# A graph network stack on one core: three-plane table blocks for the second spline layer, and the third layer's table built in the stage that finds the targets

## The chip, the cores and the metric

The kernel runs on one core of one Trainium2 chip. The metric is the device time in microseconds of one execution; lower is better.

## The reference

Four graph layers follow each other on 6250 nodes (32 features) and 100000 edges, each added to its input and layer-normed. The change touches only the first, a spline convolution with a small network that shifts the edge coordinates:

```python
def spline_basis(pseudo):               # [E, 3] in [0, 1], 5 knots a dimension
    pos = pseudo * (KS - 1)
    i0 = jnp.clip(jnp.floor(pos), 0, KS - 2)
    frac = pos - i0
    ...                                 # 8 corner weights and 8 indices into 125 knots
def spline_conv(x, row, col, basis, idx, W, b):
    z = jnp.einsum('ni,kio->nko', x, W).reshape(N * K, Fout)
    gathered = z[col[:, None] * K + idx]
    msg = jnp.einsum('es,eso->eo', basis, gathered)
    out = jax.ops.segment_sum(msg, row, num_segments=N)
    return out / jnp.maximum(deg, 1.0)[:, None] + b
h = elu(spline_conv(ones, row, col, basis, idx, stn1_w, stn1_b))   # 1 -> 64
h = elu(spline_conv(h, row, col, basis, idx, stn2_w, stn2_b))      # 64 -> 64
h = elu(h @ stn3_w + stn3_b)
t = h @ stn4_w + stn4_b
new_pseudo = clip(pseudo + t[col] - t[row], 0.0, 1.0)
basis2, idx2 = spline_basis(new_pseudo)
return spline_conv(x, row, col, basis2, idx2, conv_w, conv_b)      # 32 -> 32
```

## The kernel before

Nodes are padded to 6272 (49 tiles of 128, in 7 batches of 7), edges to 100352 (784 columns of 128, one edge a partition and column). The stages run one after the other; each is a block in which every engine has its own program, and semaphores order them. For the spline layer they are, in order of time:

- **Basis sweep.** The first 392 of 784 pair scatters run on GpSimd beside it. A pair scatter is an indirect DMA that writes 128 two-byte counts into a matrix in DRAM; later layers use it.
- **Table stage** (`stage_z` with `SplineTable`). For each node tile and each of the 5 planes of 25 knots, TensorE makes four pieces of a 128x1600 product in one of two four-bank PSUM buffers; VectorE copies pieces 0 and 2 to SBUF and ScalarE pieces 1 and 3; ScalarE then issues the store of that plane's block (800 KB, 6400 bytes a partition). Five blocks a tile, 245 stores, go to `z_stn2` (125 knots of 64 floats a node).
- **stn2 sweep** (`stage_spline_sweep` with chunks of 7 columns, in `summed_sweep`). GpSimd issues two indirect gathers a column, each of 7 consecutive knots (1792 bytes) an edge, from plane n and plane n+1. Two ring buffers alternate. VectorE weighs the 8 corners (`produce`), gives the ring back, and makes the segmented sums; ScalarE stages the gather indices when a ring comes free, spreads the decay and turns the sums for the store. Beside it the `PairTable` of the third layer is built: 56 tiles of 112 nodes, 5 planes each, two product pieces a plane on TensorE, two or four copies on ScalarE, and 224 stores of 700 KB that ScalarE issues into `z_conv`, where each row holds a knot and its neighbour in the next plane. In a sweep step of two chunks ScalarE does planes 0 to 2 after the first chunk and planes 3 and 4 after the second (`pairs.scalar`).
- **Target stage** (`stage_targets`). GpSimd issues the other 392 pair scatters. For each unit of 4 columns (7 a chunk of 28, 196 in all) TensorE counts and turns a one-hot matrix (`turn`, 8 matmuls), ScalarE copies the turned rows to SBUF as bf16 (`lo_rows`, L1834), TensorE looks the target values up (`look`, 12 matmuls), and VectorE picks them (L1795). `turned` and `found` have two PSUM buffers each, and `turn` of unit u is issued ahead of `look` of unit u-1.
- **conv sweep.** The same sweep with chunks of 28 columns and one gather of 1792 bytes an edge from `z_conv`.

The semaphores that matter below: `lo_rows_ready` (ScalarE to TensorE), `turned_ready` (back), `found_ready` and `found_free` (with VectorE), `pair_plane` and `pair_free` (TensorE and ScalarE around a plane of the pair table), `indices_staged` (ScalarE to GpSimd), `ring_free` (VectorE to ScalarE).

Of the kernel before, what the change touches and what calls it, by code (L numbers as in the profile page):

```python
# [5 lines left out]
I32 = mybir.dt.int32  # L6
BF16 = mybir.dt.bfloat16
F16 = mybir.dt.float16
ALU = mybir.AluOpType
# [5 lines left out]
P = 128  # L15


def gnn_stack_kernel(nc, t, out, stop=None):

    N, FX = t["x"].shape  # L20
# [13 lines left out]
    K3P = (KD - 1) * KD * KD  # L34
    H1 = t["L0_gnn_stn1_w"].shape[2]
# [58 lines left out]
    with ctx:  # L94
# [9 lines left out]
        z_stn2 = dram("z_stn2", [NP * K3, H1])  # L104
# [595 lines left out]
        def summed_sweep(gathers, ch, width, produce, dest, keep, tail, decay_in_psum=False, pool=None, pairs=None):  # L700

            steps = J // ch // 2
            with ExitStack() as st, nc.Block() as block:
# [27 lines left out]
                @block.tensor  # L731
                def _(pe):
                    if pairs:
                        pairs.tensor(pe)

                @block.sync
                def _(sp):
                    if pairs:
                        pairs.sync(sp)
# [15 lines left out]
                def _(a):  # L755
# [37 lines left out]
                    if pairs:  # L793
                        pairs.scalar_begin(a)
                    with a.Fori(0, steps - 1) as it:
                        for b in range(2):
                            chunk(b, it * (2 * ch) + (2 + b) * ch, it * (2 * ch) + (1 + b) * ch)
                            if pairs:
                                pairs.scalar(a, it, 3 * b, 3 + 2 * b, True)
                    chunk(0, None, J - ch)  # L800
                    if pairs:
                        pairs.scalar(a, steps - 1, 0, KD, False)
                    chunk(1, None, None)
                    if pairs:
                        pairs.scalar_end(a)
# [606 lines left out]
        def spline_setup(pseudo, w8, units, starts, dst_f):  # L1412


            with ExitStack() as st:
# [5 lines left out]
                def f(v):  # L1421
# [35 lines left out]
                    for d, s in enumerate((KD * KD, KD, 1)):  # L1457
# [3 lines left out]
                    v.tensor_copy(starts[0][:, :], ix[:, :]).then_inc(dve_step, 1)  # L1461
                    v.wait_ge(dve_step, 1)
                    v.sem_inc(dve_step, -1)
                    if len(starts) == 2:
                        v.tensor_scalar(starts[1][:, :], ix[:, :], float(KD * KD), None, ALU.add).then_inc(dve_step, 1)
                        v.wait_ge(dve_step, 1)
                        v.sem_inc(dve_step, -1)
                vector_stage(f)

        class PairTable:  # L1470

            def __init__(self, st, arr, kin, w_dram, fo, z):
                self.arr, self.kin, self.fo, self.w_dram = arr, kin, fo, w_dram
                self.nodes = NP // (J // SEVEN // 2)
                self.n_blocks = KD - 1
                self.zv = z.rearrange("(t p u) o -> p t u o", p=self.nodes, u=self.n_blocks * KD * KD)
                self.wsb = sb(st, "pair_w", [kin, K3, fo])
                self.flat = sb(st, "pair_x", [kin, NP])
                self.cell = sb(st, "pair_cell", [kin, self.nodes])
                self.blocks = [sb(st, f"pair_block{a}", [self.nodes, KD * KD, 2, fo]) for a in range(self.n_blocks)]  # L1480
                self.acc = [ps(st, f"pair_acc{n}", [P, 2, 512]) for n in range(2)]
                cuts = [0, KD * KD // 2, KD * KD]
                self.pieces = list(zip(cuts[:-1], cuts[1:]))
                self.stored = [counted(f"z_stored{a}") for a in range(self.n_blocks)]
                self.base = [k.base for k in self.stored]
                self.tiles = NP // self.nodes
                for k in self.stored:
                    k.base += 16 * (self.tiles + 1)
                self.turns = [(n, min(n + 8, NT)) for n in range(0, NT, 8)]

            def sync(self, sp):
                cut = [K3 * n // self.n_blocks for n in range(self.n_blocks + 1)]
                for a in range(self.n_blocks):
                    sp.dma_start(self.wsb[:, cut[a]:cut[a + 1], :],
                                 self.w_dram.rearrange("k i o -> i k o")[:, cut[a]:cut[a + 1], :]).then_inc(self.stored[a].sem, 16)

            def tensor(self, pe):
                for n, (lo, hi) in enumerate(self.turns):
                    if n >= 2:
                        pe.wait_ge(sem(f"pair_free{n % 2}"), 1)  # L1500
                        pe.sem_inc(sem(f"pair_free{n % 2}"), -1)
                    for k in range(lo, hi):
                        last = pe.transpose(self.acc[n % 2][0:self.kin, (k - lo) // 4, (k - lo) % 4 * P:((k - lo) % 4 + 1) * P],
                                            self.arr[:, k, :], ident[:, :])
                    last.then_inc(sem("pair_turned"), 1)
                for a in range(self.n_blocks):
                    pe.wait_ge(self.stored[a].sem, self.base[a] + 16)
                with pe.Fori(0, self.tiles):
                    pe.wait_ge(sem("pair_cell_ready"), 1)
                    pe.sem_inc(sem("pair_cell_ready"), -1)  # L1510
                    for plane in range(KD):
                        g = plane % 2
                        pe.wait_ge(sem(f"pair_free{g}"), 1)
                        pe.sem_inc(sem(f"pair_free{g}"), -1)
                        for n, (lo, hi) in enumerate(self.pieces):
                            cols = self.wsb[:, plane * KD * KD + lo:plane * KD * KD + hi, :].rearrange("i k o -> i (k o)")
                            last = pe.matmul(self.acc[g][0:self.nodes, n, 0:(hi - lo) * self.fo], self.cell[:, :], cols, start=True, stop=True)  # L1517
                        last.then_inc(sem("pair_plane"), 1)
                for g in range(2):
                    pe.wait_ge(sem(f"pair_free{g}"), 1)  # L1520
                    pe.sem_inc(sem(f"pair_free{g}"), -1)

            def next_cell(self, a, tile):
                a.copy(self.cell[:, :], self.flat[:, bass.ds(tile * self.nodes, self.nodes)]).then_inc(act_step, 1)
                a.wait_ge(act_step, 1)
                a.sem_inc(act_step, -1)
                a.sem_inc(sem("pair_cell_ready"), 1)

            def scalar_begin(self, a):
                for n, (lo, hi) in enumerate(self.turns):  # L1530
                    a.wait_ge(sem("pair_turned"), 1)
                    a.sem_inc(sem("pair_turned"), -1)
                    for k in range(lo, hi, 4):
                        w = min(4, hi - k) * P
                        last = a.copy(self.flat[:, k * P:k * P + w], self.acc[n % 2][0:self.kin, (k - lo) // 4, 0:w])
                    last.then_inc(act_step, 1)
                    a.wait_ge(act_step, 1)
                    a.sem_inc(act_step, -1)
                    a.sem_inc(sem(f"pair_free{n % 2}"), 1)
                self.next_cell(a, 0)  # L1540

            def scalar(self, a, tile, first, end, more):
                for plane in range(first, end):
                    if plane < self.n_blocks:
                        a.wait_ge(self.stored[plane].sem, tile * 16 + (16 + self.base[plane]))
                        a.sem_inc(act_step, 1)
                        a.wait_ge(act_step, 1)
                        a.sem_inc(act_step, -1)
                    a.wait_ge(sem("pair_plane"), 1)
                    a.sem_inc(sem("pair_plane"), -1)  # L1550
                    for slot in range(2):
                        if 0 <= plane - slot < self.n_blocks:
                            for n, (lo, hi) in enumerate(self.pieces):
                                last = a.copy(self.blocks[plane - slot][:, lo:hi, slot, :],  # L1554
                                              self.acc[plane % 2][0:self.nodes, n, 0:(hi - lo) * self.fo].rearrange("p (u o) -> p u o", o=self.fo))
                    last.then_inc(act_step, 1)
                    a.wait_ge(act_step, 1)
                    a.sem_inc(act_step, -1)
                    a.sem_inc(sem(f"pair_free{plane % 2}"), 1)
                    if plane > 0:  # L1560
                        lo = (plane - 1) * KD * KD
                        a.dma_start(self.zv[:, bass.ds(tile, 1), lo:lo + KD * KD, :],
# [1624 lines left out]
```

## Time and profile before

| what | us |
| --- | --- |
| median of 2 runs | 11371.64 (11367.02 to 11376.25) |
| profiled execution, span from first to last instruction | 12824.6 |
| no other time of the profiled execution is recorded | |

Stages in the profiled execution: rank (sort) 340 to 1500, basis sweep 1577 to 2100, table 2238 to 2830, stn2 sweep 2871 to 5200, target stage 5384 to 6445, conv sweep 6500 to 7560. The rest is the attention layers and the matrix layers. Times in rows are microseconds unless marked ns. DMA is the mean busy share of the 16 DMA engines; PEclk is the granted clock of TensorE as a share of full speed, 0.50 being 1.2 GHz and 1.00 being 2.4 GHz. A row of windows has the stretch, its length, busy time (and count) of PE, PEld, DVE, ACT and POOL, then PEclk, DMA share and GB/s. In a row of groups the first number pair is busy us and mean ns, then the idle time before them with what ended it. A timeline row has start, duration, engine, line.

### The profile page before, as it was taken

How to read it: one execution, taken by the hardware profiler on the slowest of the kernel's cores; microseconds unless marked ns; L12 is line 12 of the kernel's file. 1: busy time of each engine (PE TensorE's matmuls, PEld its weight loads, DVE VectorE, ACT ScalarE, POOL GpSimd, SP SyncE). 2: the span in 40 equal slices, each digit the busy share in tenths (PEclk: the TensorE clock that was granted, in tenths of full speed). 3: DMA queues.
4: the chain of work that ended last, by engine and by line, in shares of the span. 5: the costliest groups of instructions: out<-in, count | busy, mean ns of one | idle time of the engine just before them, and what ended most of it. 6: DMA issues, size and time to landing. Idle time of an engine off the chain costs nothing. (4 is left out here: it accounts for less than half of the span.)

```text
span 12824.6 us, 84874 instructions
## 1 busy us (share of the span) xinstructions
PE 3493.7 (27%) x19713; PEld 2186.6 (17%) x19713; DVE 5436.1 (42%) x7001; ACT 2482.3 (19%) x3625; POOL 6756.2 (53%) x6784
## 2 busy tenths in 40 slices
PE   4344201763333333303500010001000100005877
PEld 3222101331111111302500000001000100004544
DVE  5333485444454444303754442222222377773111
ACT  0222152432222222101200001111111134430000
POOL 2666475006666666573057767776777566661000
PEclk8555555985555555556755555555555555557899
DMA  6000021877777777200046641111111123335799
GB/s 272 2 3 3 12 106 63 345 295 230 240 238 231 238 233 233 64 0 0 0 134 188 176 108 36 34 33 27 36 33 33 26 73 93 95 98 186 320 386 360
DMA packets 587391, 1693.59 MB, mean 132 GB/s; under 512 B 268075, under 2 KB 322770, under 8 KB 569201
## 3 DMA queue, kind: packets, MB, share of 16 engines
q0 software_dynamic: 292720, 608.23, 18.6%
q1 hardware_dynamic: 230560, 722.30, 14.5%
q10 hardware_dynamic: 63952, 361.30, 7.6%
q8 instruction: 56, 0.92, 0.0%
q14 instruction: 103, 0.84, 0.0%
HBM read 1016.07 MB, written 675.24 MB: 132 GB/s over the span
## 5 line engine op out<-in xcount | busy, mean ns | idle before, releaser
L1997 POOL DMA_INDIRECT ring<-tab_gat,at x2352 | 2347.4, 998 | 928.3 <-issue 835.5
L724 POOL DMA_INDIRECT ring<-z_stn,at x1568 | 1514.8, 966 | 1506.8 <-POOLq L721 991.1
L724 POOL DMA_INDIRECT ring<-z_conv,at x784 | 794.3, 1013 | 853.9 <-POOLq L721 592.9
L1517 PE MATMUL pair_acc<-pair_w,pair_cell 32*112 32x384 f32 (+1 forms) x1120 | 806.0, 887 | 1499.7 <-issue 468.9
L578 POOL DMA_INDIRECT sorted<-rows,at x784 | 800.8, 1021 | 710.6 <-POOLq L576 477.3
L1100 POOL DMA_INDIRECT adj<-val_a,at_a x784 | 785.5, 1002 | 335.0 <-issue 255.7
L2576 PE MATMUL acc<-spot,ones 128*128 128x128 f32 x6 | 2.3, 487 | 3444.1 <-PEq L1965 2243.5
L1267 PE MATMUL acc<-tile,parts 128*96 128x448 f16 (+1 forms) x3430 | 728.5, 361 | 254.4 <-DVE parts L1191 139.2
L1916 DVE COPY corner_banks<-w 128x56 f32 (+1 forms) x140 | 35.7, 255 | 1549.5 <-issue 389.7
L2108 DVE COPY peak<-peak 128x6 f32<-128x6 f32 x112 | 21.4, 191 | 1567.3 <-DMA ring<-tab_gat,at 1521.1
L1517 PEld LDWEIGHTS pair_acc<-pair_w,pair_cell 32*112 32x112 f32 x1120 | 307.8, 295 | 1996.9 <-issue 1996.9
L2576 PEld LDWEIGHTS acc<-spot,ones 128*128 128x128 f32 x6 | 1.5, 311 | 3444.8 <-issue 3444.8
L1554 ACT COPY pair_block<-pair_acc 112x384 f32<-112x384 f32 (+1 forms) x896 | 380.8, 502 | 896.9 <-issue 438.7
L2144 DVE TENSOR_TENSOR_SCAN sums<-decay,sums 128x1176 f32<-128x1176 f32 (+1 forms) x112 | 517.3, 4619 | 29.0 <-issue 11.4
L1267 PEld LDWEIGHTS acc<-tile,parts 128*96 128x96 bf16 (+1 forms) x3430 | 403.1, 125 | 573.7 <-DMA tile<-adj 239.2
L2032 ACT ACTIVATE weights_bank<-arg 128x168 f32<-128x168 f32 (+1 forms) x112 | 31.3, 279 | 2414.3 <-issue 1966.3
L2131 DVE TENSOR_TENSOR sums<-ring,weights_bank 128x1008 f32<-128x1008 f32 (+1 forms) x112 | 430.1, 3841 | 143.5 <-issue 108.4
L1173 POOL DMA_INDIRECT own<-tab_gcn,ex_src x5 | 5.0, 991 | 907.8 <-DMA tab_gcn<-hop 601.9
L2047 ACT COPY out_rows<-sums 128x1176 f32<-128x1176 f32 (+1 forms) x112 | 443.0, 3956 | 48.9 <-ACTq L2046 16.6
L1637 PE MATMUL planes<-wsb,turned 64*128 64x384 f32 (+1 forms) x1960 | 421.5, 537 | 72.8 <-PEq L1633 72.8
L1795 DVE TENSOR_TENSOR prod<-found,hot_hi 128x588 f32<-128x588 f32 x196 | 151.1, 771 | 644.2 <-remote 306.9
L836 DVE TENSOR_TENSOR_SCAN sums<-decay,sums 128x448 f32<-128x448 f32 (+2 forms) x168 | 387.9, 2309 | 43.2 <-issue 27.3
(510 smaller groups left out, 9794.9 us busy)
## 6 DMA issues: line engine op xcount, KB each, us to landing
tile<-adj SPq DMA_DIRECT2D x490, 784.0 KB, 21.4
z_stn<-block ACTq DMA_DIRECT2D x245, 800.0 KB, 4.9
z_conv<-pair_block ACTq DMA_DIRECT2D x224, 700.0 KB
run_gat<-out_rows SPq DMA_DIRECT2D x56, 1596.0 KB
adj<-zero SPq DMA_DIRECT2D x49, 1568.0 KB
run_basis<-out_rows SPq DMA_DIRECT2D x28, 1750.0 KB
ring<-tab_gat,at POOLq DMA_INDIRECT x2352
run_gat<-out_rows SPq DMA_DIRECT2D x56, 672.0 KB
```

What stands on the lines that cost most here:

```text
L578: g.indirect_dma_start(out=dest, out_offset=bass.IndirectOffsetOnAxis(ap=at[b][:, k:k + 1], axis=0), in_=rows[b][:, k, :], in_offset=None) ...
L724: g.indirect_dma_start(out=view(bufs[b], k), out_offset=None, in_=table, in_offset=bass.IndirectOffsetOnAxis(ap=at[n][b][:, k:k + 1], axis ...
L836: v.tensor_tensor_scan(flat, decay[:, :, :].rearrange("p f j -> p (f j)"), flat, 0.0, ALU.mult, ALU.add).then_inc(dve_step, 1)
L1100: g.indirect_dma_start(out=adj, out_offset=bass.IndirectOffsetOnAxis(ap=at_a[:, k:k + 1], axis=0), in_=val_a[:, k:k + 1], in_offset=None). ...
L1267: ins = pe.matmul(acc[0:3 * w, b, 0:HW_B], parts[:, t_, :, :].rearrange("p k f -> p (k f)"), self.ring[n % RING][:, b * HW_B:(b + 1) * HW_ ...
L1517: last = pe.matmul(self.acc[g][0:self.nodes, n, 0:(hi - lo) * self.fo], self.cell[:, :], cols, start=True, stop=True)
L1554: last = a.copy(self.blocks[plane - slot][:, lo:hi, slot, :], self.acc[plane % 2][0:self.nodes, n, 0:(hi - lo) * self.fo].rearrange("p (u ...
L1637: ins = pe.matmul(self.acc[g][:, n, 0:(hi - lo) * self.fo], self.turned[rows, k, :], cols, start=True, stop=True)
L1997: g.indirect_dma_start(out=ring[b][:, k, :], out_offset=None, in_=tab_gat, in_offset=bass.IndirectOffsetOnAxis(ap=at[b][:, k:k + 1], axis= ...
L2047: a.copy(out_rows[b][:, :, 0:n_sums], sums[b][:, :, :, :].rearrange("p h f j -> p j (h f)"))
L2131: v.tensor_tensor(sums[b][:, :, 1:per_head, :], val_of(ring[b]), ex.unsqueeze(2).to_broadcast([P, NH, width, ch]), ALU.mult)
L2144: v.tensor_tensor_scan(flat, decay[:, :, :, :].rearrange("p h f j -> p (h f j)"), flat, 0.0, ALU.mult, ALU.add).then_inc(dve_step, 1)
```

## The change

Two things change.

`z_stn2` is laid out in two blocks of three planes a node (planes 0, 1, 2 and planes 2, 3, 4), each knot's three planes side by side: 150 rows of 64 floats a node instead of 125. One gather of 20 consecutive rows (5120 bytes) holds all 8 corners of an edge, so there is one gather a column, 784 instead of 1568. The table stage drains plane 2 twice, into both blocks, and stores two blocks a tile of 2400 KB each (19200 bytes a partition) from two sets of SBUF blocks. `spline_setup` gets two more small VectorE instructions for the start rows.

The pair table leaves the sweep and is built in the target stage, with 49 tiles of 128 nodes. Its two product pieces use different 32-row groups of TensorE. It has one PSUM buffer of two banks, and `turned` and `keys` give up one bank each for it. SyncE issues its stores. ScalarE and TensorE take 35 planes an iteration of 28 units, in the written-out order below.

```diff
-        def summed_sweep(gathers, ch, width, produce, dest, keep, tail, decay_in_psum=False, pool=None, pairs=None):
+        def summed_sweep(gathers, ch, width, produce, dest, keep, tail, decay_in_psum=False, pool=None):
...
                     with a.Fori(0, steps - 1) as it:
                         for b in range(2):
                             chunk(b, it * (2 * ch) + (2 + b) * ch, it * (2 * ch) + (1 + b) * ch)
-                            if pairs:
-                                pairs.scalar(a, it, 3 * b, 3 + 2 * b, True)
...
 class PairTable
+            def tensor_plane(self, pe, n):
+                k, plane = divmod(n, KD)
+                pe.wait_ge(sem("planes_free0"), 1)
+                pe.sem_inc(sem("planes_free0"), -1)
+                for m, (lo, hi) in enumerate(self.pieces):
+                    rows = slice(m * self.kin, (m + 1) * self.kin)
+                    cols = self.wsb[rows, plane, 0:hi - lo, :].rearrange("i k o -> i (k o)")
+                    pe.matmul(self.acc[:, m, 0:(hi - lo) * self.fo], self.turned[rows, k, :], cols,
+                              start=True, stop=True).then_inc(sem("plane_for_act"), 1)
...
+            def scalar_plane(self, a, it, n):
+                k, plane = divmod(n, KD)
+                if plane < self.n_blocks:
+                    a.wait_ge(self.stored[plane].sem, it * (16 * TB) + (16 * k + self.start[plane]))
...
+                a.wait_ge(sem("plane_for_act"), 2)
+                a.sem_inc(sem("plane_for_act"), -2)
+                for slot in range(2):
+                    if 0 <= plane - slot < self.n_blocks:
+                        for m, (lo, hi) in enumerate(self.pieces):
+                            last = a.copy(self.blocks[plane - slot][:, lo:hi, slot, :],
+                                          self.acc[:, m, 0:(hi - lo) * self.fo].rearrange("p (u o) -> p u o", o=self.fo))
+                last.then_inc(act_step, 1)
+                a.wait_ge(act_step, 1)
+                a.sem_inc(act_step, -1)
+                a.sem_inc(sem("planes_free0"), 1)
+                if plane > 0:
+                    a.sem_inc(sem("pair_block_full"), 1)
...
 class SplineTable
-                self.blocks = [sb(st, f"block{a}", [P, KD * KD, self.slots, fo]) for a in range(self.n_blocks)]
+                self.blocks = [[sb(st, f"block{a}{e}", [P, KD * KD, SLOTS, fo]) for e in range(2)] for a in range(2)]
...
+            def places(self, plane):
+                return [(a, plane - 2 * a) for a in range(2) if 0 <= plane - 2 * a < SLOTS]
+            def drain(self, put, k, plane, first):
+                for a, slot in self.places(plane):
+                    for n, (lo, hi) in list(enumerate(self.pieces))[first::2]:
+                        last = put(self.blocks[a][k % 2][:, lo:hi, slot, :],
+                                   self.acc[(k * KD + plane) % 2][:, n, 0:(hi - lo) * self.fo].rearrange("p (u o) -> p u o", o=self.fo))
...
 stage_targets
-                turned = [ps(st, f"turned{b}", [P, UN, P]) for b in range(2)]
+                turned = ps(st, "turned", [P, UN, P])
...
+                def planes_after(n):
+                    return range(planes * n // (4 * units), planes * (n + 1) // (4 * units))
...
                 @block.scalar
+                    with a.Fori(0, steps // 2) as it:
+                        pairs.scalar_tiles(a, it)
+                        for n in range(4 * units):
+                            b, u = n // units % 2, n % units
+                            a.wait_ge(sem("turned_ready"), 1)
+                            a.sem_inc(sem("turned_ready"), -1)
+                            a.copy(lo_rows[b][:, u * UN:(u + 1) * UN, :], turned[:, :, :]).then_inc(act_step, 1)
+                            a.wait_ge(act_step, 1)
+                            a.sem_inc(act_step, -1)
+                            a.sem_inc(sem("lo_rows_ready"), 1)
+                            if n == 0:
+                                pairs.scalar_turned(a)
+                                a.sem_inc(sem("z_tiles_ready"), 1)
+                            for m in planes_after(n):
+                                pairs.scalar_plane(a, it, m)
...
                 @block.tensor
+                            for u in range(1, units + 1):
+                                rows_taken()
+                                if u < units:
+                                    turn(b, u)
+                                look(b, u - 1)
+                                if half == 0 and u == 1:
+                                    pe.wait_ge(sem("z_tiles_ready"), 1)
+                                    pe.sem_inc(sem("z_tiles_ready"), -1)
+                                for m in planes_after(half * units + u - 1):
+                                    pairs.tensor_plane(pe, m)
```

`rows_taken` is the wait for `lo_rows_ready` that stood at the head of `look` before.

## Rows read from the trace of the kernel before

**Rows 1.** The page: span, busy time of each engine.
```profile
span 12824.6 us, 84874 instructions
...
PE 3493.7 (27%) x19713; PEld 2186.6 (17%) x19713; DVE 5436.1 (42%) x7001; ACT 2482.3 (19%) x3625; POOL 6756.2 (53%) x6784
```

**Rows 2.** Windows: stages or their steady parts; columns as told above.
```profile
2238.00:2830.00 592.00, 433.56 (x2009) 218.07 (x2009) 253.70 (x493) 237.05 (x511) 0.00 (x0) 0.90 0.85 343
2300.00:2400.00 100.00, 78.61 (x367) 39.17 (x367) 45.69 (x90) 42.67 (x93) 0.00 (x0) 0.93 0.90 365
...
3000.00:5000.00 2000.00, 696.40 (x968) 266.08 (x968) 984.55 (x1262) 517.27 (x1208) 1313.45 (x1358) 0.50 0.76 236
5384.00:5910.00 526.00, 39.20 (x297) 31.38 (x297) 30.58 (x35) 8.20 (x14) 397.58 (x392) 0.51 0.02 0
5910.00:6445.00 535.00, 293.82 (x3625) 283.96 (x3625) 357.37 (x289) 106.71 (x182) 0.45 (x1) 0.77 0.00 0
...
6600.00:7500.00 900.00, 0.00 (x0) 0.00 (x0) 441.99 (x309) 67.57 (x69) 673.61 (x666) 0.50 0.65 182
```

**Rows 3.** Groups of instructions in the stn2 sweep, 2871 to 5200.
```profile
L724 POOL DMA_INDIRECT ring<-z_stn,at x1568 | 1514.8, 966 | 1506.8 <-POOLq L721 991.1 <-issue 509.0 <-remote 6.6
L1517 PE MATMUL pair_acc<-pair_w,pair_cell 32*112 32x384 f32 (+1 forms) x1120 | 806.0, 887 | 1499.7 <-issue 468.9 <-PEq L1514 392.1 <-remote 390.1
```

**Rows 4.** Waits in that stretch, us in total, times, longest.
```profile
POOL ring L724 <- POOLq L721: 991.1, 43, 710.4
```

**Rows 5.** One source line (ScalarE's `chunk_done` increment), both sweeps; ns min/median/max.
```profile
L785 ACTq EVENT_SEMAPHORE  x112: 4/17/1380, 2908.9 to 5197.7; - x112
```

**Rows 6.** The same line, conv sweep.
```profile
L785 ACTq EVENT_SEMAPHORE  x27: 17/17/17, 6563.0 to 7545.5; - x27
```

**Rows 7.** Timeline of ScalarE, target stage, while the scatters run: start, duration.
```profile
5399.38 0.59 ACT L1834 CAST lo_rows<-turned 128x512 bf16<-128x512 f32 x1 [1.91 <-issue]
...
5655.78 0.59 ACT L1834 CAST lo_rows<-turned 128x512 bf16<-128x512 f32 x1 [55.41 <-issue]
5711.78 0.59 ACT L1834 CAST lo_rows<-turned 128x512 bf16<-128x512 f32 x1 [55.41 <-ACTq L1833]
```

**Rows 8.** Line L1834 after the scatters, 5910 to 6445.
```profile
L1834 ACT CAST lo_rows<-turned x182: 586/586/589, 5937.9 to 6438.3; 128x512 bf16<-128x512 f32 x182
```

**Rows 9.** Groups in the target stage while the scatters run.
```profile
L1100 POOL DMA_INDIRECT adj<-val_a,at_a x392 | 398.1, 1015 | 144.7 <-issue 128.4 <-SPq L1724 16.3
```

**Rows 10.** Timeline of TensorE, first units of the target stage.
```profile
5397.02 1.64 PE L1856 MATMUL found<-parts,lo_rows 128*128 128x147 bf16 x12 [0.52 <-PEq L1853]
...
5399.06 1.13 PE L1856 MATMUL found<-parts,lo_rows 128*128 128x147 bf16 x12
```

**Rows 11.** Timeline, one plane's two product pieces on TensorE.
```profile
3000.52 2.98 PE L1517 MATMUL pair_acc<-pair_w,pair_cell 32*112 32x384 f32 x4 [4.71 <-issue]
```

**Rows 12.** Timeline of ScalarE: a plane with four copies, one with two.
```profile
3507.84 1.68 ACT L1554 COPY pair_block<-pair_acc 112x384 f32<-112x384 f32 x4 [0.49 <-ACTq L1548]
3509.82 0.32 ACTq L1562 DMA_DIRECT2D z_conv<-pair_block  x1
3510.26 0.89 ACT L1554 COPY pair_block<-pair_acc 112x384 f32<-112x384 f32 x2 [0.74 <-ACTq L1550]
```

**Rows 13.** Timeline of the table stage, two planes.
```profile
2512.01 1.67 PE L1637 MATMUL planes<-wsb,turned 64*128 64x384 f32 x8 [0.25 <-PEq L1633]
...
2513.92 1.67 PE L1637 MATMUL planes<-wsb,turned 64*128 64x384 f32 x8 [0.24 <-PEq L1633]
...
2514.66 0.91 ACT L1649 COPY block<-planes 128x384 f32<-128x384 f32 x2 [1.00 <-ACTq L1694]
```

**Rows 14.** Timeline of VectorE, first and last instruction of one sweep chunk.
```profile
3504.00 0.22 DVE L1916 COPY corner_banks<-w 128x56 f32 x1 [7.35 <-DMA ring<-z_stn,at]
...
3512.14 0.95 DVE L1934 TENSOR_TENSOR sums<-corner_banks,ring 128x448 f32<-128x448 f32 x1
...
3515.34 0.22 DVE L841 COPY tail<-sums 128x64 f32<-128x64 f32 x1 [0.24 <-DVEq L839]
```

More of the change, by code:

```diff
@@ L1408, in _, with spline_setup @@
                     v.sem_inc(dve_step, -1)
-        def spline_setup(pseudo, w8, units, starts, dst_f):
+        def spline_setup(pseudo, w8, units, strides, starts, dst_f):
             with ExitStack() as st:
@@ L1491, in sync @@
[L1491 to L1521, printed above, removed]
@@ L1523, in next_cell @@
-            def next_cell(self, a, tile):
-                a.copy(self.cell[:, :], self.flat[:, bass.ds(tile * self.nodes, self.nodes)]).then_inc(act_step, 1)
+                self.zv = z.rearrange("(t p u) o -> p t u o", p=P, u=self.n_blocks * KD * KD)
+                self.tiles = sb(st, "pair_tiles", [P, TB, 2, kin])
+                self.turned = sb(st, "pair_turned", [2 * kin, TB, P])
+                self.blocks = [sb(st, f"pair_block{a}", [P, KD * KD, 2, fo]) for a in range(self.n_blocks)]
@@ new lines, in __init__ @@
+                self.pieces = [(0, KD * KD // 2), (KD * KD // 2, KD * KD)]
+                most = max(hi - lo for lo, hi in self.pieces)
+                self.wsb = sb(st, "pair_w", [2 * kin, KD, most, fo])
+                self.acc = ps(st, "pair_acc", [P, 2, 512])
+                self.stored = [counted(f"z_rows{a // 2}{a % 2}") for a in range(self.n_blocks)]
+                self.weights_on = [self.stored[plane % self.n_blocks] for plane in range(KD)]
+                self.start = [k.base + 16 * 2 * self.weights_on.count(k) for k in self.stored]
@@ L1525, in next_cell, with scalar_tiles @@
+            def scalar_tiles(self, a, it):
+                a.copy(self.tiles[:, :, :, :], self.arr[:, bass.ds(it * TB, TB), :].unsqueeze(2).to_broadcast([P, TB, 2, self.kin])).then_inc(act_step, 1)
                 a.wait_ge(act_step, 1)
                 a.sem_inc(act_step, -1)
[L1527 to L1536, printed above, removed]
+                a.sem_inc(sem("z_tiles_in"), 1)
@@ L1537, in scalar_begin @@
+            def scalar_plane(self, a, it, n):
+                k, plane = divmod(n, KD)
+                if plane < self.n_blocks:
+                    a.wait_ge(self.stored[plane].sem, it * (16 * TB) + (16 * k + self.start[plane]))
+                    a.sem_inc(act_step, 1)
                     a.wait_ge(act_step, 1)
                     a.sem_inc(act_step, -1)
[L1539 to L1562, printed above, removed]
-                                    self.blocks[plane - 1][:, :, :, :].rearrange("p u s o -> p u (s o)").unsqueeze(1)
-                                    ).then_inc(self.stored[plane - 1].sem, 16)
-                if end == KD and more:
-                    self.next_cell(a, tile + 1)
@@ L1938, in whole @@
                 def whole(buf, k):
+                    if triple:
+                        return buf[:, k, :, :].rearrange("p u o -> p (u o)")
                     return buf[:, k, :, :, :].rearrange("p u s o -> p (u s o)")
[L1941 to L1944 removed]
+                summed_sweep([(z, starts, ring, whole)], ch, fo, produce, run, keep, tail)
         def node_sums(st, run, end_i, open_, tail, width):
```

273 lines of the change are left out of this document (137 added, 136 removed).

## The prediction

> **What bounds the kernel now.** I read the page first, for the span [rows 1], then windows by stage [rows 2], then groups and waits inside the stages that the diff touches, then timelines for single steps. The change touches the table stage, the stn2 sweep and the target stage, together 4.0 ms of the 12.8 ms span.
>
> One thing has to be settled before any row is used. The profiled span is 12824.6 [rows 1], the median 11371.64: the profiled execution is 1453 us longer. The rows say where. ScalarE's one-tick semaphore increment at L785 takes 17 ns in all 27 records of the conv sweep [rows 6], but up to 1380 ns in the stn2 sweep [rows 5]. In the target stage TensorE starts its first two units 2.0 us apart, with the scatters already running [rows 10]; a little later two units lie 56.0 us apart [rows 7]. A unit is 20 matmuls with 20 weight loads, so 1.40 us an instruction, which no data wait explains. When the scatters end, the same unit takes 500.4/182 = 2.75 us [rows 8]. Both appear only where an engine makes many records while GpSimd issues indirect DMAs. I take these as the profiler's own cost: records back up, and the engine is held. Behind these rows: the Trainium skill, "NOTIFIC — the notification-queue block", section 7.1, says that the block's internal pipeline always back-pressures its producers and can throttle an engine. The rows agree with that reading; no run here shows it.
>
> So the undisturbed stages are worked out thus. **stn2 sweep:** GpSimd's 1568 gathers, 1514.8 busy plus 509.0 of issue = 2024 [rows 3]; at 0.946+0.30 us each, 1954. The remaining waits for staged indices in the stretch (991.1 less the 710.4 before it) [rows 4] come from ScalarE being held. I take 1985, against 2320 profiled. DMA is close behind: share 0.76 at 236 GB/s [rows 2]. **Target stage:** 196 x 2.75 + 10 of start = 550, against 1054 profiled; the scatters, 392 x 1.27 = 497 [rows 9], fit under it. **Table stage:** 583 in both, since no gather runs there. The first two account for 335 + 504 of the 1453.
>
> **Table stage after.** It is bound by stores and TensorE together: a plane starts every 1.91 us [rows 13], and the best stretch moves 365 GB/s at share 0.90 [rows 2]. Before: 6272 x 125 x 256 B = 200.7 MB, 550 us at 365 GB/s, plus 33 of start and batch changes. After: x150 = 240.8 MB, 660 at 365 GB/s, or 595 at the full share (365/0.90 = 405 GB/s); plus 33. Draining plane 2 twice adds 0.91 us of ScalarE copies a tile [rows 13], under 13 us of store time a tile. So +45 to +110, taken +95 (nearer the rate that was reached). The two extra VectorE instructions of the set-up are about 2 us.
>
> **stn2 sweep after.** GpSimd: 784 x 1.246 = 977, no bound any more. VectorE: a chunk runs from 3504.00 to 3515.56 [rows 14], with its semaphores 12.0 us; x112 = 1347. DMA: a column moves 128 x 5120 = 655 KB in and 33 KB of sums out, 688 KB. The price of rows of 5120 bytes is not in the trace, so from both sides. At 405 GB/s: 1.70 us a column, 1332. At the conv sweep's efficiency (182/0.65 = 280 GB/s for rows of 1792 bytes) [rows 2]: 2.46, 1926. Between them: that sweep loses 246 KB/280 - 246 KB/405 = 0.27 us a gather; if this is paid by the gather and not by the byte, 1.97, or 1545 at full share and 1717 at 0.90. The ring's loop fits: produce holds a ring 9.2 us [rows 14], re-staging and first data take some 3 more, under one chunk's transfer of 13. I take 1600, nearest to the per-gather reading, since longer rows mean fewer breaks. So -385 (-65 to -540).
>
> Beside it: the skill's "DMA: Bandwidth & Descriptors", section Bandwidth, gives 358 GB/s as a core's HBM limit; by it the column costs 1.92 us and the sweep 1507. The best stretch here, 365 GB/s, is slightly over it.
>
> **Target stage after.** This is the term that decides. The chain of one unit, in program order: ScalarE copies `lo_rows` of unit n and signals; TensorE, behind `rows_taken`, issues `turn` n+1, `look` n, and then a plane of the pair table; ScalarE waits for that plane, drains it, and only then copies `lo_rows` n+1; TensorE's next instruction waits for that copy. `planes_after` gives each unit at least one plane and seven of 28 a second. There is one pair buffer, so a second plane also waits for the first's drain. Behind ScalarE's wait stands `lo_rows`, behind TensorE's the next `turn`: nothing of the two engines overlaps. Before, two `turned` buffers and no planes let the copy lie under TensorE's work.
>
> At 1.2 GHz, TensorE: signal and take 0.25; `turn` 0.60, `look` 1.46 (from 5397.02 to the next turn at about 5398.46, and from there to 5399.06 [rows 10]); the plane. Its two pieces took 2.98 us on one row group [rows 11]; on two groups they should run together, as the table stage's four pieces do (1.67 us at clock 0.93 for twice the columns [rows 2, 13]), so 1.65. Sum 3.96. ScalarE: a drain of four copies 1.71, of two 0.93 [rows 12], mean of a tile (3 x 1.71 + 2 x 0.93)/5 = 1.40; semaphores 0.3; `lo_rows` 0.59 and 0.1. Sum 2.4. The extra quarter plane: (1.75 + 1.65)/4 = 0.85. Together 7.2 us a unit. At 2.4 GHz TensorE's part shrinks to 2.5 and the unit to 5.6. Which clock: TensorE would be busy about half the time, between the sweep (35% busy, 0.50) and the scatter-free stretch (55%, 0.77) [rows 2]; I take 0.65, 6.4 us. 196 x 6.4 + 7 x 3 for turning a batch of tiles = 1275. VectorE's 2.7 us a unit hides. The stores, 157 MB in 1275 us, meet idle DMA (share 0.00 to 0.02 [rows 2]) on SyncE, where nothing else queues. So +725: +550 at the full clock, +900 at 1.2 GHz.
>
> The skill's "TensorE: Matmul & The Clock Gate", Part 3, says matmuls in different row groups run concurrently; rows 13 agree. Serial pieces would put 1.25 x 1.3 us on a unit, +320.
>
> **Sum.** +95 - 385 + 725 = +435, less some 5 for the pair work's start: 11372 + 430 = 11,800 us, 3.8% slower. Against the profiled execution's own time it comes out otherwise: table +95; the sweep 2320 to about 1650, as ScalarE's records are halved; in the target stage the scatters cover 7 units at 50 x 1.4 = 70 us and 189 follow at 6.4, 1720, +665. Span about 12,910.
>
> **Rivals.** (1) *The holds are real* and are in the timed runs too; then the 1453 us lie elsewhere. The profiled sum holds: +90, 11,460, no measurable change. For it: the rows show holds and no row shows their absence. Against: 1.4 us an instruction on TensorE with idle DMA. Chance 0.15. (2) *The engines overlap after all* (faster): the target stage is then bound by ScalarE's own work, 0.9 + 1.25 x 1.7 = 3.0 us a unit, 590 + 21, +60; with the sweep at 1500 the total is 11372 + 80 - 485 + 60 = 11,030. Against it: the written order. Chance 0.10. (3) *Gathers pay by the byte:* the sweep stays at 1926 or above (540 MB at the 236 GB/s it now moves gives 2290); 95 - 60 + 725 = +760, 12,130, or 12,500. Chance 0.13. (4) The forecast: 0.62. What turns it is the target stage's unit: at 4.2 us (196 x 4.2 + 21 = 845, +295) the three terms cancel.
>
> **How the numbers follow.** 2% of the median, 227 us, is about what a measurement of this kernel can tell. Faster by over 2% (under 11,144): rival 2 and a scrap of the forecast, 0.12. Within 2%: rival 1 and the forecast's low edge (+50: 45 - 540 + 550), 0.20. Slower: the rest, 0.68. The forecast's own terms give +50 to +945. The range 11,420 to 12,200 takes in rival 1 and the nearer form of rival 3, and leaves out rival 2 and the far ends.
>
> **What the changed profile would show.** Table stage 640 to 700 us with DMA share near 0.9. Sweep: 784 gathers, the wait for indices on GpSimd large, VectorE waiting for the ring, DMA over 300 GB/s. Target stage after the scatters: `lo_rows` copies 5.6 to 7.2 us apart, TensorE's wait on ScalarE before `turn`, ScalarE's wait on the plane, clock 0.5 to 0.8; during them, units some 70 us apart. Wrong would be: units 3 us apart, a plane of 3 us, or a sweep at 240 GB/s. If both stages are as forecast and the timed difference is far from +430, the reading of the 1453 us is what failed.

## The result, and the profile after

| | us |
|---|---|
| before, median of 2 runs | 11371.64 |
| after, median of 2 runs (11870.6 to 11871.58) | 11871.09 |
| ratio after / before | 1.0437, interval 1.0406 to 1.0467 |
| profiled execution, before / after | 12824.6 [rows 1] / 11869.8 |

The kernel is 4.4% slower; 11,800 was forecast. The first thing to see is in the last line: the profiled execution of before is 1453 us longer than its median, that of after agrees with its median. Set side by side, the two profiles say that the change saves 955 us; the timed runs say that it costs 499.

The page of after, its span, busy times, two groups and the two tables' stores (KB each, us to landing):

```profile
span 11869.8 us, 82214 instructions
...
PE 3154.5 (27%) x19573; PEld 2100.9 (18%) x19573; DVE 5479.1 (46%) x7071; ACT 2450.8 (21%) x3451; POOL 5886.5 (50%) x6000
...
L726 POOL DMA_INDIRECT ring<-z_stn,at x784 | 772.1, 985 | 1515.0 <-POOLq L723 1294.3
...
z_stn<-block ACTq DMA_DIRECT2D x98, 2400.0 KB, 14.9
z_conv<-pair_block SPq DMA_DIRECT2D x196, 800.0 KB, 3.4
```

Against [rows 1], GpSimd has 784 instructions fewer and 870 us less of busy time (782 against the second profile of before, below). Its gathers cost as much each as before, 985 ns against 966 [rows 3], though each brings 5120 bytes a partition where one of before brought 1792 (7 knots of 256 bytes). Its waits for staged indices at L723 come to 1294.3 us. One of them, 742.2, ends with the first gather and lies ahead of the sweep; 552 lie in it.

```profile
POOL ring L726 <- POOLq L723: 1294.3, 111, 742.2
```

The three stages that the change touches, by windows of after (columns as in [rows 2]): table stage, stn2 sweep, target stage.

```profile
1982.00:2592.00 610.00, 429.24 (x1996) 256.79 (x1992) 296.04 (x588) 275.40 (x606) 0.00 (x0) 0.87 0.91 386
2653.00:4199.00 1546.00, 0.00 (x0) 0.00 (x0) 1121.92 (x1437) 187.81 (x332) 772.10 (x784) 0.50 0.92 347
4387.00:5874.00 1487.00, 873.87 (x4945) 527.64 (x4942) 374.53 (x281) 458.70 (x1000) 389.46 (x386) 0.51 0.27 108
```

The table stage stores at 386 GB/s. The sweep is short and moves 347 GB/s at share 0.92; GpSimd is busy for only half of it. The target stage is the long one: no engine in it is busy for more than 59% (TensorE, 874 of 1487 us), DMA is at 0.27, and TensorE's granted clock is 0.51, its lower level of 1.2 GHz. With nothing busy, the waits have to say who waits for whom (engine, group, releaser: us in total, times, longest), 4380 to 5890:

```profile
DVE prod L1780 <- DVEq L1778: 1091.3, 196, 9.2
ACT pair_block L1548 <- ACTq L1544: 932.4, 245, 4.7
...
PE counts L1843 <- PEq L1858: 404.1, 160, 3.3
```

ScalarE waits 245 times, 3.8 us each, for a plane at L1544, and TensorE 2.5 us each for ScalarE's copy of `lo_rows` before it may `turn`. VectorE's long wait is the result, not the cause: its product follows `look`. One unit in the timeline (start, duration; idle before in brackets) shows the loop:

```profile
5304.48 0.59 ACT L1827 CAST lo_rows<-turned 128x512 bf16<-128x512 f32 x1 [0.28 <-ACTq L1826]
...
5305.33 0.23 PE L1843 MATMUL counts<-hot_hi,hot_lo 128*128 128x49 bf16 x1 [2.13 <-PEq L1858]
...
5305.93 1.69 PE L1852 MATMUL found<-parts,lo_rows 128*128 128x147 bf16 x12
...
5307.55 1.76 PE L1517 MATMUL pair_acc<-pair_w,pair_turned 32*128 32x384 f32 x4
5307.77 0.77 DVE L1780 TENSOR_TENSOR prod<-found,hot_hi 128x588 f32<-128x588 f32 x1 [5.34 <-DVEq L1778]
5309.43 1.68 ACT L1548 COPY pair_block<-pair_acc 128x384 f32<-128x384 f32 x4 [4.37 <-ACTq L1544]
5311.46 0.58 ACT L1827 CAST lo_rows<-turned 128x512 bf16<-128x512 f32 x1 [0.35 <-ACTq L1826]
...
5312.31 0.24 PE L1843 MATMUL counts<-hot_hi,hot_lo 128*128 128x49 bf16 x1 [3.00 <-PEq L1858]
```

Read down: copy, `turn`, `look`, plane, drain, copy. Nothing of ScalarE lies beside a matmul of TensorE: 0.85 us from the copy's start to `turn`, 3.98 on TensorE, 0.12 of signal, 1.68 of drain and 0.35 before the next copy make the 6.98 us. Over the stage:

```profile
L1827 ACT CAST lo_rows<-turned x196: 585/585/586, 4387.3 to 5864.4; 128x512 bf16<-128x512 f32 x196
```

1477.1/195 gaps is 7.6 us a unit. Of these gaps 147 belong to units with one plane and are 6.65 us on average; most units with two planes take 10.0, and the batch starts up to 13.2.

### The profile page after: what moved, and what is told of

Same layout as the page of the kernel before. It is cut to its first block and busy times, and to the rows that moved or that the text cites. A ratio compares the mean times of both kernels' runs of the same rounds, so it can differ in the third digit from the quotient of the medians.

```text
span 11869.8 us, 82214 instructions
## 1 busy us (share of the span) xinstructions
PE 3154.5 (27%) x19573; PEld 2100.9 (18%) x19573; DVE 5479.1 (46%) x7071; ACT 2450.8 (21%) x3451; POOL 5886.5 (50%) x6000
## 5 line engine op out<-in xcount | busy, mean ns | idle before, releaser
L2007 POOL DMA_INDIRECT ring<-tab_gat,at x2352 | 2240.8, 953 | 813.3 <-issue 720.6
L726 POOL DMA_INDIRECT ring<-z_stn,at x784 | 772.1, 985 | 1515.0 <-POOLq L723 1294.3
L726 POOL DMA_INDIRECT ring<-z_conv,at x784 | 766.6, 978 | 1281.9 <-POOLq L723 1030.3
L1548 ACT COPY pair_block<-pair_acc 128x384 f32<-128x384 f32 (+1 forms) x784 | 334.0, 504 | 932.4 <-ACTq L1544 932.4
L753 ACT COPY at<-cell 128x7 int32 (+2 forms) x140 | 28.0, 200 | 2061.5 <-ACTq L768 1945.7
L1517 PE MATMUL pair_acc<-pair_w,pair_turned 32*128 32x384 f32 x980 | 426.4, 939 | 101.4 <-PEq L1513 101.4
L1637 DVE COPY block<-planes 128x384 f32<-128x384 f32 x588 | 296.0, 552 | 336.1 <-DVEq L1656 336.1
```

What stands on the lines that cost most here:

```text
L726: g.indirect_dma_start(out=view(bufs[b], k), out_offset=None, in_=table, in_offset=bass.IndirectOffsetOnAxis(ap=at[n][b][:, k:k + 1], axis ...
L1517: pe.matmul(self.acc[:, m, 0:(hi - lo) * self.fo], self.turned[rows, k, :], cols, start=True, stop=True).then_inc(sem("plane_for_act"), 1)
L1637: last = put(self.blocks[a][k % 2][:, lo:hi, slot, :], self.acc[(k * KD + plane) % 2][:, n, 0:(hi - lo) * self.fo].rearrange("p (u o) -> p ...
L2007: g.indirect_dma_start(out=ring[b][:, k, :], out_offset=None, in_=tab_gat, in_offset=bass.IndirectOffsetOnAxis(ap=at[b][:, k:k + 1], axis= ...
```

## The experiments

All timed ratios are against the kernel before, timed again with each group of runs: its median is 11355.25 us beside b, a and c and 11357.69 beside d, e and g, where it was 11371.64 beside after. The stages of every run, from its first to its last table copy, gather and product, in us:

| run | table | sweep | target | span | timed, ratio to before |
|---|---|---|---|---|---|
| before, profile of [rows 1] | 559 | 2311 | 1042 | 12824.6 | 11371.64 |
| e0_before_again | 560 | 2053 | 530 | 11378.8 | 11380.54 (one run) |
| after | 609 | 1545 | 1477 | 11869.8 | 1.0437 |
| b_pairs_alone | 560 | 2040 | 1472 | 12300.6 | 12304.8, 1.0835 (1.0817 to 1.0854) |
| a_blocks_stores | 609 | 1800 | 530 | 11198.1 | 11204.1, 0.9877 (0.9852 to 0.9902) |
| c_drain_late | 609 | 1546 | 964 | 11347.9 | 11356.19, 1.0001 (0.9991 to 1.001) |
| d_no_planes | 609 | 1546 | 535 | 10958.7 | 10949.4, 0.9636 (0.9619 to 0.9654) |
| e_pairs_beside_gather | 607 | 1809 | 530 | 11236.4 | 11211.26, 0.9869 (0.9851 to 0.9887) |
| g_products_twice | 608 | 1546 | 1817 | 12221.8 | 12225.19, 1.0765 (1.0742 to 1.0788) |

**e0_before_again** is the kernel before, unchanged, for a second profile. It asks whether the 1453 us belong to the kernel.

> The kernel before, unchanged, profiled once more. Theory 1 (the 1453 us between its profiled span and its median were the recording's own hold on engines that make many records while GpSimd issues indirect DMAs): either the span is again some 12,800 with the same 56 us units, or, if the holds do not recur, it is 11,370, with the stn2 sweep at 1950 to 2050, the target stage at 550 to 600 and the semaphore increment of the sweep at 17 ns throughout. Theory 2 (the holds are real and the missing time lies elsewhere): a span near 11,370 would still show the sweep at 2300 and the target stage at 1050.

```profile
span 11378.8 us, 84818 instructions
```

ScalarE's semaphore increment, and the `lo_rows` copies of the whole target stage:

```profile
L785 ACTq EVENT_SEMAPHORE  x168: 17/17/17, 1358.3 to 6483.3; - x168
```

```profile
L1834 ACT CAST lo_rows<-turned x196: 586/586/589, 4840.3 to 5371.3; 128x512 bf16<-128x512 f32 x196
```

The same increments that reached 1380 ns [rows 5] take 17 ns in all three sweeps, and the units lie (5371.3 - 4840.3)/195 = 2.72 us apart with the scatters running, where they lay 56 apart [rows 7]. The same three stages by windows:

```profile
1992.00:2552.00 560.00, 428.86 (x1994) 215.12 (x1990) 250.16 (x490) 235.00 (x508) 0.00 (x0) 0.92 0.87 357
2602.00:4656.00 2054.00, 780.01 (x1155) 320.96 (x1152) 1127.02 (x1443) 595.45 (x1392) 1520.17 (x1568) 0.50 0.83 264
4840.00:5375.00 535.00, 314.78 (x3916) 304.07 (x3914) 375.25 (x307) 114.91 (x196) 409.10 (x386) 0.79 0.02 0
```

This is the profile of before to compare with. The group of its gathers (busy, mean | idle before, releasers) closes the sweep's account: 1520.2 busy and 499.0 of issue are 2019 of 2053 us.

```profile
L724 POOL DMA_INDIRECT ring<-z_stn,at x1568 | 1520.2, 969 | 1214.6 <-POOLq L721 715.0 <-issue 499.0 <-ACTq L762 0.6
```

Theory 1 stands in its second form, the holds do not recur; the stages lie just outside what it gave, the sweep 3 us above 2050 and the target stage 20 us below 550. Between the two profiles of before lie 1446 us. The stn2 sweep accounts for 258 of them and the target stage for 512. The rest lies where the change touches nothing: 270 ahead of the table stage, 346 behind the conv sweep, and some 60 in and between the stages from the table to the conv sweep.

**b_pairs_alone** does the second half of the change alone: after, with before's `spline_setup`, `SplineTable` and stn2 sweep put back.

```diff
-        z_stn2 = dram("z_stn2", [NP * K3T, H1])
+        z_stn2 = dram("z_stn2", [NP * K3, H1])
+                    if len(starts) == 2:
+                        v.tensor_scalar(starts[1][:, :], ix[:, :], float(KD * KD), None, ALU.add)...
```

> The second half of the change alone: z_stn2 in 125 rows a node with two gathers a column, as before; the pair table in the target stage, as after. Theory 1 (the target stage is a serial chain of 7.5 us a unit, and the sweep is held by GpSimd's 1568 gathers at 1.246 us with or without the pair table beside it): target stage 1484, sweep 1960, total 11372 + 930 - 20 = 12,280, 8% slower. Theory 2 (the pair table beside the sweep cost it DMA time, and moving it frees some 300 us): total 11,970 or below.

```profile
2601.00:4641.00 2040.00, 0.00 (x0) 0.00 (x0) 1126.77 (x1443) 199.64 (x443) 1517.38 (x1568) 0.50 0.67 189
```

Theory 1 stands, though its sweep of 1960 us was 80 too short: by the second profile of before a gather takes 2019/1568 = 1.288 us and not 1.246. Without the pair table the sweep is 13 us shorter, 2040 against 2053, though DMA falls from 264 to 189 GB/s: the bound was GpSimd's two gathers a column, and beside them the pair table was all but free. In the target stage the same table costs 942 us (1472 - 530). Moving it costs 8.35% by itself.

**a_blocks_stores** does the first half: the three-plane table and one gather, with before's target stage. Before's pair table didn't fit in SBUF beside the larger ring, so beside the sweep stand only its stores; its products and copies are left out, and `z_conv` gets a block of zeros.

```diff
+                for plane in range(max(first, 1), end):
+                    a.wait_ge(self.stored[plane - 1].sem, tile * 16 + self.base[plane - 1])
+                    a.dma_start(self.zv[...], self.block[...]).then_inc(self.stored[plane - 1].sem, 16)
```

> The first half of the change with the pair table's traffic left beside the sweep: three-plane blocks, one 5120-byte gather a column, target stage as before; the pair table's products and copies are left out, and its 224 stores of 700 KB go out in their old places from a block of zeros, so z_conv holds zeros. (The whole pair table does not fit in SBUF beside the larger ring.) Theory 1 (with one gather a column the sweep is bound by DMA, at the 347 GB/s that it reaches in the changed kernel, so the stores cost their bytes): sweep (514 + 26 + 157 MB)/347 = 2010, total 11372 + 45 + 20 = 11,430, no gain from the merged gather as long as the stores are beside it. Theory 2 (the merged gather is what makes the sweep fast, and stores hide): sweep 1560 to 1650, total 11,000 or below.

```profile
2666.00:4466.00 1800.00, 0.00 (x0) 0.00 (x0) 1117.32 (x1432) 187.62 (x331) 773.63 (x784) 0.50 0.99 385
```

The result lies between the two theories, 1.2% under before where theory 1 had no gain and theory 2 over 3%. The sweep takes 1800 us, with share 0.99 at 385 GB/s: here DMA is the bound, and the price of one gather with the pair stores beside it is bytes. Theory 1 had the mechanism and too low a rate. It had taken what after's sweep moves, 347 GB/s, for the limit, but after's sweep stops short of that: its share is 0.92, and its VectorE waits 111 times 2.4 us for the ring (269.3 us). The Trainium skill, "DMA: Bandwidth & Descriptors", section Bandwidth, gives 358 GB/s as a core's HBM limit, and calls about that each core's share with both cores of a domain streaming; its own measurements, up to 425 GB/s, are of a core alone. The 385 here and the 386 of the table stage, on one core, lie 8% above the first figure and below the second.

**c_drain_late** is after with ScalarE's order changed: ScalarE copies `lo_rows` of a unit first and drains the plane of the unit before it second, so that the drain lies beside TensorE's work.

```diff
                                 a.sem_inc(sem("z_tiles_ready"), 1)
-                            for m in planes_after(n):
-                                pairs.scalar_plane(a, it, m)
+                            else:
+                                for m in planes_after(n - 1):
+                                    pairs.scalar_plane(a, it, m)
+                        for m in planes_after(4 * units - 1):
+                            pairs.scalar_plane(a, it, m)
```

> The changed kernel, with ScalarE's drains of a unit's planes put one unit later, behind the next lo_rows copy; TensorE's program is unchanged. Theory 1 (what costs is the order: TensorE waits for a drain and a copy that wait for TensorE): TensorE's own work bounds the unit, 0.1 + 0.6 + 1.6 + 1.25 x 1.7 = 4.4 us at 1.2 GHz or less at a higher clock, target stage 650 to 880, total 11,050 to 11,270. Theory 2 (what costs is the work that was added, or one PSUM buffer for the turned rows): the stage stays above 1300, total above 11,690.

```profile
4380.00:5370.00 990.00, 801.46 (x4955) 494.51 (x4955) 387.65 (x299) 458.69 (x1000) 402.01 (x391) 0.58 0.42 163
```

In its timeline the drain and the next `look` run together, which after's written order rules out:

```profile
4999.52 1.76 PE L1517 MATMUL pair_acc<-pair_w,pair_turned 32*128 32x384 f32 x4
...
5001.40 1.69 ACT L1548 COPY pair_block<-pair_acc 128x384 f32<-128x384 f32 x4 [1.05 <-ACTq L1544]
...
5001.84 1.69 PE L1855 MATMUL found<-parts,lo_rows 128*128 128x147 bf16 x12
...
5003.43 0.58 ACT L1827 CAST lo_rows<-turned 128x512 bf16<-128x512 f32 x1 [0.35 <-ACTq L1826]
...
5003.46 1.75 PE L1517 MATMUL pair_acc<-pair_w,pair_turned 32*128 32x384 f32 x4
```

The stage falls from 1477 to 964 us and the kernel by 515, to before's time. The engines, instructions and bytes are the same, so 513 of the 947 us that the move costs come back with ScalarE's order alone. Of these, TensorE's own busy time gives 72 (874 to 801 us for the same work, as its clock goes from 0.51 to 0.58); the rest was waiting. The stage stayed above theory 1's range (650 to 880), and the kernel above its 11,050 to 11,270: with the chain open TensorE comes nearest to a bound, busy 801 of 990 us against 315 in the target stage of before, and its clock is 0.58, not the higher level. Its longest wait that is left is the one for the one pair buffer before a plane:

```profile
PE pair_acc L1517 <- PEq L1513: 126.0, 87, 2.4
```

**d_no_planes** leaves out the planes' products and drains; SyncE stores blocks of zeros, so `z_conv` holds zeros. It asks what the stores and the new order of `turn` and `look` cost by themselves.

```diff
-                            for m in planes_after(n):
-                                pairs.scalar_plane(a, it, m)
...
-                                for m in planes_after(half * units + u - 1):
-                                    pairs.tensor_plane(pe, m)
```

> The changed kernel without the 245 planes' products and drains in the target stage: blocks of zeros are stored in their place on the same queue, so z_conv holds zeros; the single PSUM buffer for the turned rows, the turning of a batch's tiles and the stores stay. Theory 1 (the planes' chain is the whole loss): unit 2.7 to 3.0 us, target stage 530 to 600, total 10,920 to 11,000, clock back near 0.79. Theory 2 (the single buffer and TensorE's earlier wait for the copied rows cost on their own): unit over 3.5 us, target stage over 690, total over 11,080.

```profile
4400.00:4850.00 450.00, 281.87 (x3297) 261.76 (x3298) 307.56 (x232) 104.10 (x180) 339.51 (x316) 0.81 0.92 351
```

Theory 1's numbers. The stores (196 of 800 KB, 161 MB with a KB of 1024 bytes; the prediction and the expectations say 157) go out at 351 GB/s beside GpSimd's scatters, and the stage is 535 us against 530. So the stores, the single `turned` buffer and `rows_taken` cost 5 us between them while no planes are built; the other 942 come with products and drains in that order. Whether a second `turned` buffer would save more beside the planes was not run. Its 10,949 us is also about the least that this change could give, with the building hidden altogether.

**g_products_twice** issues each plane's two matmuls twice. In a serial chain all of the second product shows.

```diff
+                for m, (lo, hi) in enumerate(self.pieces):
+                    pe.matmul(self.acc[:, m, ...], self.turned[rows, k, :], cols, start=True, stop=True)
                 for m, (lo, hi) in enumerate(self.pieces):
                     pe.matmul(self.acc[:, m, ...], ...).then_inc(sem("plane_for_act"), 1)
```

> The changed kernel with every plane's two products issued twice into the same PSUM banks. Theory 1 (the product lies in series on the unit's chain): 245 planes at 1.4 to 1.6 us more, target stage +340 to +390, total 12,210 to 12,260. Theory 2 (TensorE waits for ScalarE anyway, and the product hides in that wait): under +100.

```profile
4380.00:6230.00 1850.00, 1209.14 (x5930) 730.47 (x5930) 394.13 (x304) 459.06 (x1001) 395.23 (x392) 0.51 0.23 87
```

The stage grew from 1477 to 1817 us, by 340, or 1.39 us for each of the 245 planes, and the timed kernel by 354. That is less than the 1.76 us of a pair of pieces alone, since two pairs behind each other overlap at their ends: in the timeline the second pair starts 1.44 us after the first. The longer stage has the same clock, 0.51. TensorE's busy time grew by some 335 us (874 to 1209), so nearly all of the added work shows in the stage's length: the path had no slack to take it up.

**e_pairs_beside_gather** takes the good half and puts the building back where it was hidden: after's table and gather, before's target stage, and the pair table in its new form (two row groups, one PSUM buffer, tiles of 128) in the stn2 sweep, 35 planes over every 16 chunks, its stores issued by ScalarE.

```diff
+                                chunk(k % 2, ...)
+                                for m in range(n_pl * k // per_b, n_pl * (k + 1) // per_b):
+                                    pairs.scalar_plane(a, it, m)
```

> The three-plane blocks and the one gather of the changed kernel, the target stage of the kernel before, and the whole pair table back beside the stn2 sweep, in its new form (49 tiles of 128 nodes, two row groups, one PSUM buffer of two banks, which fits), with 35 planes spread over every 16 chunks and the stores issued by ScalarE. Theory 1 (the sweep is bound by DMA bytes, and TensorE and ScalarE are idle enough there to hide the pair table): sweep 1800 to 1850 as with the stores alone, total 11,200 to 11,270, 1% faster than the kernel before. Theory 2 (ScalarE's plane work delays the staging of indices, as one ring is always waiting): each chunk loses 1 to 3 us, sweep 1950 to 2100, total 11,350 to 11,500, no gain.

```profile
2655.00:4480.00 1825.00, 433.30 (x1009) 135.37 (x1009) 1131.10 (x1444) 524.94 (x1120) 770.88 (x783) 0.50 0.96 378
4690.00:5215.00 525.00, 307.50 (x3826) 297.07 (x3825) 368.59 (x300) 111.99 (x191) 401.31 (x380) 0.79 0.02 0
```

Theory 1 again: the sweep 1809 us, the target stage 530 as before, the kernel 1.3% under before and 5.6% under after (11211.26 against 11871.09). That is the version that beats both. The interval leaves out a ratio of 1, though the gain is under the 2% that the prediction took as what can be told. (The window above begins 18 us ahead of the first gather.) The planes are really built here, and the sweep is only 9 us longer than with the stores alone (a_blocks_stores): products and drains are hidden, the bytes are not.

## Why the prediction was right, and where its terms were off

Against the second profile of before, the stages account for the result: table 609 - 560 = +49, sweep 1545 - 2053 = -508, target 1477 - 530 = +947, together +488; the spans differ by 491 and the timed medians by 499.

**The reading of the 1453 us: right, and shown for this execution.** The same kernel profiled again has a span of 11378.8, increments of 17 ns and units of 2.72 us. Rival 1, that the holds are real, falls. Wrong was the part that made them a property of every profile: after's span was forecast at 12,910 with units of 70 us, and its profile has none of it. The prediction placed 839 of the 1453 in the two stages and said nothing of the rest; between the two profiles they hold 770 of 1446. Why one execution had the holds stays open. The Trainium skill, "NOTIFIC — the notification-queue block", section 7.1, says that the record-writing block can hold back the engines that feed it; that would fit the one execution, and no run here shows it.

**The sweep before: 1985 forecast, 2053 measured.** GpSimd was the bound as said; the estimate took 0.946 us a gather from undisturbed records where the mean is 0.969, 36 us of the 68, and 0.30 of issue where it is 0.318 a gather, 28 more.

**The sweep after: 1600 forecast, 1545 measured.** The bounds for 5120-byte rows were 1.70 and 2.46 us a column. The measured one is 1546/784 = 1.97 at share 0.92. That this is the per-gather reading's value at full share is luck: at share 0.92 that reading gives 1545/0.92 = 1680 us. Nor is DMA slow inside a chunk: in two windows of 7 us (from 3504 and from 3518) it moves 421 and 420 GB/s at full share. It falls to 160 GB/s at share 0.6 around the start of a chunk's gathers (3511 to 3513, 3538 to 3541), and 248 of 1535 windows of 1 us have a share under 0.8. So the ring's loop, which the prediction let fit under the transfer, does show, 2.4 us of VectorE's waiting a chunk; what would close the gap was not tested. Rival 3 falls. With the term before it: -508 where -385 stood. Two slips carry nothing: 12.0 us x 112 is 1344, not 1347, and the term's low end of -540 follows from none of its readings (1332 us would be -653).

**The table: +95 forecast, +49 measured.** Mis-sized is the rate. The forecast went by the 365 GB/s of before's best stretch for both kernels; the stage's mean went from 357 to 386 GB/s. Stores of 2400 KB and the second set of blocks came together, and which of them raised it was not tested.

**The target stage: +725 forecast, +947 measured.** The mechanism stands by four results: the timeline shows the loop closed; c_drain_late opens it and gets 513 us back; g_products_twice adds to it and pays in full; d_no_planes leaves only 5 us to the rest without planes. Rival 2, that the engines overlap after all, falls for this order, and c_drain_late shows how far it would have carried: not to 600 us, since TensorE itself then needs 801. The pieces on two row groups ran together as forecast, 1.76 us for a plane against 2.98 on one [rows 11]. Mis-sized is the clock: I took 0.65, by interpolating between stages by TensorE's busy share, and it was 0.51. At 1.2 GHz I had worked out 7.2 us a unit, a stage of 1432 and +900 (1432 less 550 is 882); measured are 7.6, 1477 and +947, with 530 and not 550 before. The second plane adds what was forecast, 3.4 us; the one-plane unit takes 6.65 where the terms give 6.36. The interpolation was the step that failed. The busy share doesn't order the clocks of these stages: 0.79 at 59% busy (before's target stage), 0.51 at 59% (after's), 0.58 at 81% (c_drain_late), 0.87 to 0.92 at 70 to 77% (table stages).

The errors partly cancel, +222 on the target stage against -46 and -123 on the others: the total was 70 us low. Had the middle value of the clock come true, the forecast would have been 150 us too high.

**Where the gain went.** The gather's gain is real but never 508 us on its own: of it, 253 remain once the pair stores are back in the sweep (a_blocks_stores), because those 161 MB had been free only while GpSimd was the bound. The other 255 come only with the stores out of the sweep, and the change put the table into a stage with idle DMA and idle share on every engine, and the store part of that did work, at 5 us (d_no_planes). The build part cost 942, since the written order made the two engines take turns: 513 of it came back with ScalarE's order, and most of the rest is TensorE's added work at the lower clock (c_drain_late).

## What to carry to other kernels

- Set the profiled span against the timed median before using a row of it. Where they differ by per cents, look for records of fixed one-tick instructions that have grown; a second profile of the same kernel settles it.
- Busy shares don't say that a stage has room. Where two engines hand work back and forth in a written order that leaves nothing of one beside the other, as here, the work that is added to either is added to the time. Draining one unit late opened the loop here with a few lines.
- When one change joins a saving and a move, time the halves: -1.2% (with the stores beside it) and +8.4% here, and the best version takes the first and leaves the second.

## What the runs showed of the hardware

- The cost of an indirect gather on GpSimd hardly changed with its row: 985 ns for 5120 bytes a partition, 969 for 1792. The idle time put down to issue is 0.33 us a time in both (220.7 us in 673 times, 499.0 in 1507).
- DMA reached 385 GB/s at share 0.99 with gathers of 5120-byte rows and 700 KB stores together (a_blocks_stores), and 386 at 0.91 with 2400 KB stores alone (after's table stage). For 7 us inside a chunk of after's sweep it reached 421 at full share.
- TensorE's granted clock was 0.51 to 0.58 in every target stage with the f32 products of 32 rows in it, up to 81% busy, and 0.79 to 0.81 in those without, at 59 to 63% busy. What in the work makes that difference was not tested.
- One profiled execution in the nine here, of the same kernel that otherwise profiles at its timed length, was 13% longer, with TensorE held 1.4 us an instruction while GpSimd issued scatters.
